# The first router of a fused attention and feed-forward kernel run in parts, with swapped PSUM bank pairs and a re-ordered first hidden block

## What is computed

```
x = x + tanh(g_xattn) * attention(layernorm(x), ctx, ctx)      # 16 heads of 16, rotary positions, softmax over 154 keys
x = x + tanh(g_ffn)   * ffn(layernorm(x))

def mole(x, W, b, A, B, Rw):                                    # E = 3 experts of rank R = 8
    gates = softmax(x @ Rw)                                     # the router
    base  = x @ W + b
    z     = x @ A[e]                       for each expert
    return base + 1/8 * sum_e (z[e] * gates[e]) @ B[e]

def ffn(x):
    h = relu(mole(x, W1, b1, A1, B1, R1))                       # 256 -> 1024
    return mole(h, W2, b2, A2, B2, R2)                          # 1024 -> 256
```

## Time and profile before

| | us |
|---|---|
| median of 3 runs | 538.13 |
| those runs | 537.85, 538.13, 1131.6 |
| the profiled execution, whole time | 536.79 |
| its span, first to last instruction | 535.0 |

### The profile page before, as it was taken

The page is one execution under the profiler, slowest core; times in us unless marked ns, Lnnn a source line. Parts: engine busy times, 40 slices in busy tenths (PEclk is TensorE's granted clock), DMA queues, the critical chain, the costliest instruction groups (busy, mean ns, idle before and its releaser), DMA issues.

```text
span 535.0 us, 7892 instructions
## 1 busy us (share of the span) xinstructions
PE 486.0 (91%) x3032; PEld 355.9 (67%) x3032; DVE 380.1 (71%) x896; ACT 205.3 (38%) x325; POOL 70.4 (13%) x118
## 2 busy tenths in 40 slices
PE   4459839999999999999999999999999999999897
PEld 3335337748885596748885596748885596739696
DVE  4746586948886688849796688848796778826543
ACT  6333512571236412571236422571236422461230
POOL 6373020010202010010202010010202010101000
PEclk9956977999999999999999999999999999999899
DMA  8561140107001140207001140207001040200011
GB/s 311 142 192 43 39 122 1 53 1 196 8 20 62 40 121 1 93 1 196 7 31 51 44 117 1 93 1 197 6 40 42 8 113 1 82 0 1 1 41 39
DMA packets 20385, 34.30 MB, mean 64 GB/s; under 512 B 5588, under 2 KB 9500, under 8 KB 20220
## 3 DMA queue, kind: packets, MB, share of 16 engines
q1 hardware_dynamic: 12704, 16.28, 11.1%
q10 hardware_dynamic: 7644, 17.52, 10.4%
HBM read 14.28 MB, written 4.19 MB: 35 GB/s over the span
## 4 chain that ended last, share of the span: by engine, by line
PE 79%; DVE 13%; ACT 3%; issue 2%; DMA 2%; POOL 1%; SPq 0%; ACTq 0%; DVEq 0%
PE psF L1219 16%; PE psF L1182 14%; PE psX L1202 7%; PE psO L1301 5%; PE psX L1278 4%; PE psX L1096 4%; PE psX L1113 4%; DVE max_t L828 4%; PE psF L1293 3%; PE psO L1293 3%; PE psF L1188 2%; PE psX L1273 2%; PE psX L1154 2%; DVE xT_lo L761 2%; PE psX L1182 1%
## 5 line engine op out<-in xcount | busy, mean ns | idle before, releaser
L828 DVE TENSOR_REDUCE max_t<-psX 128x4 fp32r<-128x616 f32 x128 | 99.3, 795 | 13.4 <-PE psX L1202 12.0
L1202 PE MATMUL psX<-km,qT 128*128 128x308 f32 x256 | 64.8, 342 | 13.7 <-DMA qT<-probs 10.9
L1219 PE MATMUL psF<-w_hi,h_hi 128*128 128x284 f32 (+1 forms) x240 | 72.5, 302 | 0.0
L1219 PE MATMUL psF<-w_lo,h_hi 128*128 128x284 f32 (+1 forms) x240 | 70.3, 293 | 0.0
L1219 PE MATMUL psF<-w_hi,h_lo 128*128 128x284 f32 (+1 forms) x240 | 70.1, 292 | 0.0
L621 ACT ACTIVATE probs<-psX 128x1024 f32<-128x1024 f32 x64 | 64.2, 1026 | 12.4 <-PE psX L1278 12.4
L1202 PEld LDWEIGHTS psX<-km,qT 128*128 128x128 f32 x256 | 48.3, 206 | 28.3 <-DMA qT<-probs 11.4
L539 ACT ACTIVATE h_hi<-psF 128x512 fp32r<-128x512 f32 x59 | 34.4, 594 | 54.3 <-PE psF L1188 54.3
L1219 PEld LDWEIGHTS psF<-w_hi,h_hi 128*128 128x128 f32 x240 | 45.1, 188 | 5.9 <-issue 5.9
L398 POOL TENSOR_TENSOR x<-x,tab 128x256 f32<-128x256 f32 x32 | 22.3, 730 | 181.0 <-DMA x<-in_x_dram 181.0
L1182 PE MATMUL psF<-xT_lo,w_hi 128*128 128x512 f32 x118 | 45.7, 401 | 0.0
(11 more groups left out here) (170 smaller groups left out, 885.5 us busy)
## 6 DMA issues: line engine op xcount, KB each, us to landing
qT<-probs SPq DMA_DIRECT2D x32, 256.0 KB
qT<-probs ACTq DMA_DIRECT2D x16, 256.0 KB
x<-in_x_dram ACTq DMA_DIRECT2D x8, 512.0 KB, 3.3
x_ln<-in_x_dram ACTq DMA_DIRECT2D x7, 512.0 KB, 4.1
out_dram<-x ACTq DMA_DIRECT2D x7, 512.0 KB, 3.0
turn<-in_turns_dram SPq DMA_DIRECT2D x2, 512.0 KB, 7.4
heads_t<-in_w_dram SPq DMA_DIRECT2D x1, 1024.0 KB, 9.9
heads_t<-in_w_dram SPq DMA_DIRECT2D x1, 994.0 KB, 7.3
```

The lines of the kernel that those rows point to most:

```text
L828: V.tensor_reduce(max_t[:, k, half, :].rearrange("p (h g) -> p g h", h=2)[:, 2 * j:2 * j + 2, :], psX[:, 2 * j:2 * j + 2, 0:2 * S].rearran ...
L1202: ins = mm(psX[:, g % 4, 0:2 * S].rearrange("p (h s) -> p h s", h=2), qT[:, g, tokens(k)], km[:, g, :, 0:S], start=True, stop=True)
L1219: ins = mm(out_bank(d, k)[:, cs], a[:, m, tokens(k)], w[:, m, cs], start=m == 0 and i == 0, stop=m == HT - 1 and i == 2)
```

## The change

- `router1` is split: for each of xT_hi and xT_lo, `router_part` waits for one half f of it and runs the matmuls for that half. In all steps but LAST two matmuls of hidden block 0 (xT_hi with w1_hi, f = 0 and 1) stand between the two parts.
- z goes to bank 1 of psX (bank 3 at LAST, as before). The bank pairs of `max_scores`, `reduce_max`, `scores` and the exponentials are swapped (even i: banks 2 and 3; odd i: banks 0 and 1), and q of every chunk from 1 on goes to banks 2 and 3.
- `max_scores(c, 0)` stands behind `router1`, and the other four matmuls of hidden block 0 in one piece behind it. `max_scores(c, 2)` stands behind `out_lora(e, 1)`; each later one is one slot earlier in the loop, and only `max_scores(15)` is left behind it, ahead of `hidden_lora(7)`.
- On DVE `reduce_max(c, 0)` stands between `gates1_shift` and `finish(e, u, 2)`; the others are one slot earlier, so that `reduce_max(15)` comes before `h_low(6)`.

No instruction is added or taken away. The diff, cut:

```diff
@@ -164,7 +164,11 @@
 
         def q_bank(c, s):
 
-            return psX[:, s + 2 if c == 1 else s, :]
+            return psX[:, s + 2 if c else s, :]
+
+        def router_bank(d):
+
+            return psX[:, 3 if d is LAST else 1, :]
 
         def hidden_bank(d, m):
 
...
                             act.wait_ge(pv_ps.sem, pv_ps.at(c, n // 4 - 1))
-                    nc.scalar.activation(dst, psX[:, 2 * (i % 2):2 * (i % 2) + 2, :], ACT.Exp).then_inc(sc_exp.sem, 1)
+                    nc.scalar.activation(dst, psX[:, 2 * (1 - i % 2):2 * (1 - i % 2) + 2, :], ACT.Exp).then_inc(sc_exp.sem, 1)
...
@@ -823,7 +827,7 @@
                                        op1=ALU.subtract).then_inc(w1_lo_s.sem, 1)
 
             def reduce_max(c, i):
-                half, k, j = i // 8, i % 8 // 2, i % 2
+                half, k, j = i // 8, i % 8 // 2, 1 - i % 2
                 dve.wait_ge(max_ps.sem, max_ps.at(c, i + 1))
...
@@ -877,7 +881,7 @@
 
 
                 dve.wait_ge(z1_ps.sem, z1_ps.at(d))
-                z = psX[:, 3, 0:P]
+                z = router_bank(d)[:, 0:P]
                 V.transpose(zc[:, :, :].rearrange("p k z -> p (k z)"), z).then_inc(g1_v.sem, 1)
                 dve.wait_ge(g1_v.sem, g1_v.at(d, 1))
...
@@ -949,19 +953,20 @@
                         reduce_max(c, i)
                 else:
                     gates1_shift(d)
+                    reduce_max(c, 0)
                     if full:
                         finish(e, u, 2)
                     gates1_weigh(d)
-                    reduce_max(c, 0)
                     if full:
                         finish(e, u, 3)
                     reduce_max(c, 1)
+                    reduce_max(c, 2)
                     for m in range(HT):
                         if m < HT - 1:
-                            reduce_max(c, 2 * m + 2)
+                            reduce_max(c, 2 * m + 3)
                         h_low(d, m)
-                        if m < HT - 1:
-                            reduce_max(c, 2 * m + 3)
+                        if m < HT - 2:
+                            reduce_max(c, 2 * m + 4)
 
                 dve.wait_ge(maxT_ps.sem, maxT_ps.at(c))
                 V.tensor_scalar(max_f[:, 1, :], psO[0:H // 2, :], -1.0, None, ALU.mult).then_inc(maxT_s[1].sem, 1)
...
@@ -1137,23 +1142,27 @@
                                  start=f == 0, stop=f == FT - 1)
                 ins.then_inc(v_ps.sem, 1)
 
+            def router_part(d, a, done, first_term):
+
+                for f in range(FT):
+                    pe.wait_ge(done.sem, done.at(d, f + 1))
+                    for k in range(TT):
+                        z = router_bank(d)[32 * k:32 * k + 32, 0:P]
+                        ins = mm(z, a1_sb[:, f, :], a[:, f, tokens(k)].bitcast(F32),
+                                 start=first_term and f == 0, stop=not first_term and f == 1)
+                return ins
+
             def router1(d, second=False):
 
-                pe.wait_ge(x2T_hi_s.sem, x2T_hi_s.at(d))
-                pe.wait_ge(x2T_lo_s.sem, x2T_lo_s.at(d))
                 if second:
                     pe.wait_ge(a1_loaded.sem, 16)
                     for n in ("w1", "w2a", "w2b", "lora1", "lora2"):
                         pe.wait_ge(w_lo[n].sem, 1)
                     pe.wait_ge(pv_t.sem, pv_t.at(d))
-                n = 0
-                for a in (xT_hi, xT_lo):
-                    for f in range(FT):
-                        for k in range(TT):
-                            z = psX[32 * k:32 * k + 32, 3, 0:P]
-                            ins = mm(z, a1_sb[:, f, :], a[:, f, tokens(k)].bitcast(F32), start=n == 0, stop=n == 3)
-                        n += 1
-                ins.then_inc(z1_ps.sem, 1)
+                router_part(d, xT_hi, x2T_hi_s, True)
+                if d is not LAST:
+                    hidden_main(d, 0, second, 0, 2)
+                router_part(d, xT_lo, x2T_lo_s, False).then_inc(z1_ps.sem, 1)
 
             def lora1_operand(d):
...
@@ -1162,7 +1171,7 @@
                     ins = nc.tensor.transpose(o_ps[:, k].bitcast(F32R), zs[:, k, :], ident_r[:, :])
                 ins.then_inc(z1T_ps.sem, 1)
 
-            def hidden_main(d, m, second=False, parts=(0, 1)):
+            def hidden_main(d, m, second=False, first=0, end=6):
 
                 if d is LAST:
...
@@ -1171,13 +1180,13 @@
                         pe.wait_ge(g1_v.sem, g1_v.at(d, 1))
                     elif m == 7:
                         pe.wait_ge(w1_lo_s.sem, w1_lo_s.at(d, 1))
-                elif parts[0] == 0:
+                elif first == 0:
                     if m >= 3:
                         pe.wait_ge(w1_lo_s.sem, w1_lo_s.at(d, m - 2))
                     elif not second:
                         pe.wait_ge(y_out.sem, y_out.at(d - 1, m + 2))
                 ops = [(a, w, f) for a, w in ((xT_hi, w1_hi), (xT_lo, w1_hi), (xT_hi, w1_lo)) for f in range(FT)]
-                for n in range(3 * parts[0], 3 * parts[-1] + 3):
+                for n in range(first, end):
                     a, w, f = ops[n]
                     mm(hidden_bank(d, m), w[:, f, P * m:P * m + P], a[:, f, :], start=n == 0, stop=False)
...
@@ -1337,30 +1346,29 @@
                     if full:
                         out_tile(e, 3, HT - 2, HT)
                     pe.wait_ge(x1_s.sem, x1_s.at(d))
+                    router1(d, second)
                     max_scores(c, 0)
-                    router1(d, second)
-                    hidden_main(d, 0, second, (0,))
+                    hidden_main(d, 0, second, 2)
                     if full:
                         lora2_operand(e, 1)
                     max_scores(c, 1)
                     if full:
                         out_lora(e, 1)
-                    hidden_main(d, 0, second, (1,))
+                    max_scores(c, 2)
                     hidden_main(d, 1, second)
                     lora1_operand(d)
                     for m in range(2, HT):
-                        max_scores(c, 2 * m - 2)
-                        hidden_main(d, m, second, (0,))
+                        max_scores(c, 2 * m - 1)
+                        hidden_main(d, m, second, 0, 3)
                         if m == 2:
                             hidden_lora(d, 0)
-                        max_scores(c, 2 * m - 1)
+                        max_scores(c, 2 * m)
                         if m == 5:
                             max_transposed(c, 0, False)
-                        hidden_main(d, m, second, (1,))
+                        hidden_main(d, m, second, 3)
                         hidden_lora(d, m - 1)
-                    max_scores(c, 14)
+                    max_scores(c, 15)
                     hidden_lora(d, 7)
-                    max_scores(c, 15)
                 scores(c, 0)
                 max_transposed(c, 1, first)
                 scores(c, 1)
```

More of the change, by code:

```diff
@@ L1272, in scores @@
                             o = (P + 32) * (2 * n + k) + (-32, 32)[hh] * k
-                            ins = mm(psX[:, 2 * (i % 2) + hh, :], kr[rows, o:o + P], qT[rows, 2 * n + k, :],
+                            ins = mm(psX[:, 2 * (1 - i % 2) + hh, :], kr[rows, o:o + P], qT[rows, 2 * n + k, :],
                                      start=k == 0, stop=k == 3)
@@ L1277, in scores @@
                         rows = slice(HR * hh, HR * hh + HR)
-                        ins = mm(psX[:, 2 * (i % 2) + hh, :], km[rows, n // 2, hh, 0:P], qT[rows, n // 2, :],
+                        ins = mm(psX[:, 2 * (1 - i % 2) + hh, :], km[rows, n // 2, hh, 0:P], qT[rows, n // 2, :],
                                  start=True, stop=True)
```

## The result

The changed kernel takes 532.34 us (median of 4 runs) where the kernel before takes 538.27 us; the ratio is 0.9877, with a 95% interval of 0.9849 to 0.9905. Run again later beside other kernels it gave 530.93 us and 0.9865 (0.9837 to 0.9892). It is faster by 1.2 to 1.4%, 6 to 7 us; the forecast was 533.3 us. Its profiled execution took 530.21 us with a span of 528.4 us, 6.6 us less than the span before.

A forecast was written before the change was run, and what follows sets the result against it. PE, 79% of the chain, was taken as the bound, so gains come only where it waits. Full steps 3.0, c = 1 0.8 and LAST 1.0 sum to 4.8 us off 538.13, giving 533.3 us; range 530.8 to 536.5.

The forecast's parts named there:

- the clock dip at LAST goes: Rival: the stretch at about half clock behind the router at LAST disappears, saving 1.7 us more, 531.6 us; 25%.
- Edit 1: Router run as its halves come, full step: lora2_operand still at 266.29, but three hidden matmuls (0.70 us) more done.
- Edit 3: First maximum placed in VectorE's 0.66 us idle, full step: weighing not delayed; without this cover, up to 0.71 us later.
- Edit 4: PE stands 0.7 us before max_scores(3), until 270.53; later loop slots 0.39 us later, with one max_scores less in the loop.
- Edit 5: End of the loop: scores(0) at 285.09, next transposes at 287.07 for 287.58; 0.5 us per full step.
- The bounds given with it: Limits of the gain per full step: 0.1 us below, 0.75 us above.
- Size per step: Gain of each full step, c = 2 to 7: 0.5 us, 3.0 us for six.
- c = 1: Step without chunk e: idle before the router (0.53 us) and before scores(0) (0.33 us) goes; 0.8 us gained.
- LAST: Router's hi half runs in PE's 0.95 us idle; out_lora starts at 499.12, not 500.11: 1.0 us gained.
- VectorE gives only a part: Rival: reduce_max(0) ends late or the loop's h_low wait grows; 0.1 us per full step, 535.7 us; 20%.
- the change does nothing: Rival: time saved at the front stands again as idle before max_scores(3); 538 us; 7%.
- Slower by the clock: Rival: new 0.7 us idle before max_scores(3) drops the clock, 1.7 us each fall, up to 543.5 us; 4%.

## Why the prediction was right or wrong

**The sum.** Forecast 4.8 us, of them 3.0 in the full steps, 0.8 at c = 1 and 1.0 at LAST. Measured in the pair of profiled executions 6.6: 3.37, 0.89 and 2.34. The time came out 1 us below the forecast, between the likeliest case and the rival in which the clock dip at LAST goes (531.6 us), and in the profiled pair that rival is what happened. Without the clock the traces give 3.37 + 0.80 + 0.65 = 4.8 us, the sum as forecast. That it fits so closely is luck in part: the full steps were put 0.37 us too low and LAST 0.35 us too high, and the two cancel.

**Edit by edit in a full step**, on the clock of the earlier trace rows (after plus 2.06):

| | forecast | measured |
|---|---|---|
| router's low half done, max_scores(0) | 264.75 | 265.00 |
| lora2_operand | 266.29 | 266.31 |
| first maximum starts | 266.78 | 266.79 |
| residual behind it starts | 267.52 | 267.52 |
| max_scores(2) | 267.64 | 267.63 |
| lora1_operand | 269.45 | 269.55 |
| max_scores(3) | 270.53 | 270.53 |
| max_scores(15) | 284.56 | 284.52 |
| scores(0) | 285.09 | 285.14 |
| next transposes | 287.07 | 287.06 |

- *Edit 1, nothing earlier at lora2_operand*: right; max_scores(0) comes 0.25 us later than forecast, inside the slack (0.10 of it stands before the first record, 263.07 where 262.97 was forecast). The run with the router in parts alone shows what the sum implied and did not say: by itself it brings nothing in a full step. What it missed is the place of the wait: finish(2) holds the bank of hidden block 1. In the change itself max_scores(2) stands in that gap, so the term didn't bite.
- *Edit 3, the cover*: right. Without the cover the price was forecast as up to 0.71 us for the weighing; taken away in the other direction (the maximum behind the weighing, max_scores(2) left early) it is 1.5 us per step, and 3.1 where the clock falls.
- *Edit 4, what is late next*: right in place and time. The wait before max_scores(3) ends at the forecast 270.53. PE's wait there was given as 0.7 us and is 0.57 by the trace, because lora1_operand came 0.1 us later.
- *Edit 5, the loop's end*: right, 0.52 us at the transposes. The run without the slot shift shows that the shift itself is worth 0.07 us: my text let it look like more. The bounds given with it are rounded: by their own terms they are 0.13 and 0.73 us, and the low end of the range is 531.0 and not 530.8.
- *Size per step*: 0.5 forecast, 0.56 measured over six, 0.53 in step c = 4.
- *c = 1*: 0.8 forecast, 0.89 in this pair for all that stands ahead of c = 2. Whole starts can't tell it: they differ by more than that between two executions of one kernel (131.55 and 132.32 us for the changed kernel, 132.44 and 134.16 for the kernel before). But this pair has its half-clock stretches in the same places (granted clock 0.66 over 70 to 90 us in both), and from the start of xT_lo in c = 1 to the next project_out it takes 132.44 - 80.56 = 51.88 us before and 131.55 - 80.47 = 51.08 after: 0.80 us.
- *LAST*: the term that was mis-sized. The forecast of the place was right: out_lora at 499.12, 1.55 us behind the transposes at 497.57, and 1.56 measured. But the 500.11 that it was compared with lay at half clock; at full clock it is 2.21 us behind the transposes and not 2.54. So the order is worth 0.65 us and not 1.0, and the rival in which the clock dip goes counted the other 0.33 us twice. The other 1.7 us of the tail are the clock.

**The rivals.** *The clock dip goes*: it did in both profiled executions of the changed kernel, and the time agrees. The mean granted clock of the timed executions is 0.963 or 0.964 after, and 0.957 to 0.961 before, so (1 - clock) times the span, the time that the clock costs where PE has work throughout, is some 19.5 us after and 21 to 23 us before: one or two such stretches more. Not all of them need be at LAST: the second profiled execution of the kernel before has more half clock in its start too (granted clock 0.54 over 24 to 54 us, 0.60 in the first), and it stands 1.7 us later at c = 2. But the reason that I gave, PE's extra work in the idle time before the router, is not the cause, or not alone: with that work taken out the clock stayed up in two executions of two. *VectorE gives only a part* and *the change does nothing*: no; every full step gained. *Slower by the clock*: not at a wait of 0.57 us, in any of the six steps, over which the granted clock is 1.00; yes at 2.54 us, in four of six. By the rule of the Trainium skill's page "TensorE: Matmul & The Clock Gate", section "A second HAM failure mode: psum-queue depth-cycling", read as the prediction reads it (it gives no length of gap), the small gaps would have been enough. Here they were not.

## What to carry to other kernels

When two engines hand work to each other, time saved on the one in front of a common wait can be worth nothing until the other one's order is changed too: look for idle time of the *other* engine that is nearly as long as an instruction it does later (here 0.66 us before a residual, and a 0.71 us maximum). Then look at once for the wait that stands next and put independent work of the waiting engine into it: that gave another 0.68 us per step, more than the change had. Where a term of the sum is read off two rows at different clocks, work it out at one of them first, and price the clock by itself.

## What the runs showed of the hardware

A wait of 2.54 us on TensorE, with 2.6 of four microseconds idle in the step shown, was followed by a stretch at the lower clock in four steps of six and by none in two, in one and the same execution; each stretch cost 1.6 us (steps longer by 3.1 and by 1.5 us). Idle pieces of 0.22, 0.56 and 0.86 to 0.95 us within three microseconds were followed by such a stretch in two executions of two of one kernel and in none of two of another. So the same or nearly the same idle time can go either way, and 1.7 us of a comparison between two kernels can be that alone; steps cut at the same instruction, with the granted clock beside them, told the two apart where whole times did not.
